# Attention kernel on one NeuronCore: another place for the full-array matmul, another order of SyncE's transfers

## The chip, the cores and the metric

The kernel runs on one core of a Trainium2 chip. The metric is the device time of one execution in microseconds (us), the median of the runs shown. Engines are named as the profile does: PE is TensorE (PEld its weight loads), DVE VectorE, ACT ScalarE, POOL GpSimd, SP SyncE, which here issues nearly all DMA transfers (its queue is SPq).

## The reference, cut to what matters

An image tensor `x` of 8 x 128 x 32 x 32 goes through six blocks, each added to its input: window attention with a depthwise convolution, a gated convolution, attention over all tokens, a mixture of experts with GELU, local attention, a mixture of experts with SiLU. The change touches the first and the third:

```python
# window attention: for each of two shifts and each of two halves of the channels
qw = _to_windows(q, nh, hs, nw, ws, HEADS) * scale      # windows of 128 tokens, 8 heads of 8
attn = softmax(einsum('whqc,whkc->whqk', qw, kw))
ow = einsum('whqk,whkc->whqc', attn, vw) + lw
...
# token attention: 1024 tokens, 16 heads of 8
attn = softmax(einsum('bhqd,bhkd->bhqk', q, k))
out = einsum('bhqk,bhkd->bhqd', attn, v)
return out.reshape(b, n, c) @ w_proj + b_proj
```

## The kernel before, in words

Each block is a stage with a barrier behind it. In both attention stages every engine runs its own program written out by hand, and semaphores tie them together; nothing reorders the work. The heads lie in four row groups of 32 partitions (`j` = 0 to 3), so that four small matmuls can run side by side.

**Window attention** (`window_attention`) works on 8 images of four stacks (`u` = 0 to 3; a stack is one shift and one half of the channels), each stack of four steps (`n`), 16 steps an image. **Token attention** (`token_attention`) has 8 images of eight groups (`g`) of eight steps, 64 steps an image. A step of TensorE's program is, in both:

- wait for `st_free[0]` (ScalarE has read the first score buffer); the full-array matmul `fill_array` (L368), 128 x 128 weights, 512 columns, whose result is thrown away: it is written to the half of the score buffer `st_ps` that real scores overwrite next;
- scores of the first pair of row groups (L558 in window attention, L945 in token attention), then maxima scores of two row groups for a stack or group two ahead (L542, L932), each waiting for a free one of the three buffers of `mx_ps` (`mx_free`);
- in one step of each stack or group the transpose of the split maxima (L548, L937);
- wait for `st_free[1]`; scores of the second pair; two more maxima scores;
- the values matmuls of the step before (L571, L959).

ScalarE takes two exponentials a step (L643, L1048) and now and then copies finished outputs (L636, L1032). VectorE takes four reductions a step (L667, L1073), copies the transposed maxima to `mT` (L671, L1082), in token attention reduces them once more (L1078), and inverts the denominators (`invert`, L678 and L1088). GpSimd splits the maxima (`split_max`), expands the values (`expand_v`), and adds finished images to `X` (`finish`, `normalise`, `add`).

The order around the change, in the window attention's SyncE program, one round for each stack `u`: `load_den` (L467, the denominators of the stack before, after waiting for ScalarE's copy), `load_qk` (L453, four transfers of 192 KB for the next image's stack `u-1`), a wait for VectorE's copy of the turned maxima, `load_rows` (L461, two transfers that put them under the queries of the stack after this one; TensorE waits for them at that stack's first step, `rows_loaded`), `regroup` (L476, eight transfers of finished outputs), `load_v` (L457). In rounds 1 and 3 `spread` follows: it waits for `invert`, stores the inverses to DRAM (L484), waits, and reads them back to many partitions (L488, two transfers of 256 KB). In token attention the reciprocal of the image before stands after step 4 of VectorE's program:

```python
if n == 4 and kind != "first":
    invert(i - 1)
```

Of the kernel before, what the change touches and what calls it, by code (L numbers as in the profile page):

```python
# [365 lines left out]
def fill_array(nc, out, ident, rows):  # L366

    nc.tensor.matmul(out, ident[:], rows, start=True, stop=True)  # L368
# [8 lines left out]
def window_attention(chip, X, qk_scr, v_scr, d_scr, ident, identf):  # L377
# [11 lines left out]
    U, S, STEPS, TURN = 4, 2, 16, 1  # L389
# [25 lines left out]
    with chip.stage() as ctx:  # L415
# [19 lines left out]
        rows_loaded, v_loaded, den_loaded, rb_loaded, regrouped, st_ready, st_free = ([chip.sem(s) for _ in range(2)] for s in (  # L435
            "rows_loaded", "v_loaded", "den_loaded", "rb_loaded", "regrouped", "st_ready", "st_free"))
# [11 lines left out]
        with nc.Block() as block:  # L448
            @block.sync
            def _(sp):  # L450
                def load_qk(i, u):
                    for j in range(4):
                        sp.dma_start(QK[32 * j:32 * j + STACK, u].rearrange("p o s n -> p o (s n)"),  # L453
                                     qk_scr[i, u, :, :, j].rearrange("o r s n -> r o (s n)")).then_inc(qk_loaded[u], 16)

                def load_v(i, u):
                    sp.dma_start(VS[:, u % 2], v_scr[i, u]).then_inc(v_loaded[u % 2], 16)  # L457

                def load_rows(u):
                    for c in range(2):  # L460
                        sp.dma_start(QS[STACK + c:C:32, u].rearrange("j s n -> j (s n)"),  # L461
                                     mT[64 * c:64 * c + 64, u % 2]).then_inc(rows_loaded[u % 2], 16)

                def load_den(i, u):

                    sp.wait_ge(o_free, i * STEPS + (4 * u + 5))
                    sp.dma_start(DEN[:, u // 2, u % 2], OR[D:C:32, u % 2].rearrange("j s n -> j (s n)")).then_inc(den_loaded[u % 2], 16)  # L467

                def regroup(i, u):

                    sp.wait_ge(x_done, i * 2 + (u // 2 + 2))
                    sp.wait_ge(o_free, i * STEPS + (4 * u + 5))
                    for j in range(4):
                        for s in range(2):
                            at = 64 * (u % 2) + 2 * j + s
                            sp.dma_start(ON[at:64 * (u % 2) + 64:8, u // 2], OR[32 * j:32 * j + D, u % 2, s]  # L476
                                         ).then_inc(regrouped[u % 2], 16)

                def spread(i, h):

                    count = i * 2 + (h + 2)
                    sp.wait_ge(x_done, count)
                    sp.wait_ge(inverted, count)
                    sp.dma_start(d_scr[i, h].rearrange("a p n -> p a n"), RD[:]).then_inc(rd_stored, 16)  # L484
                    sp.wait_ge(rd_stored, i * 32 + (16 * h + 32))
                    for part in range(2):
                        src = d_scr[i, h, part].rearrange("(s a) n -> s (a n)", s=8)
                        sp.dma_start(RB[64 * part:64 * part + 64, h],  # L488
                                     src.unsqueeze(0).to_broadcast([D] + list(src.shape))).then_inc(rb_loaded[h], 16)

                sp.wait_ge(ones_set, 1)
                load_qk(0, 0)
                load_v(0, 0)
                load_qk(0, 1)
                load_v(0, 1)
                load_qk(0, 2)
                load_qk(0, 3)
                sp.wait_ge(mx_free, 20 + 1 + 3)
                load_rows(0)
                sp.wait_ge(va_done, 1)  # L500
                load_v(0, 2)

                def image(i, kind):
                    for u in range(U):
                        if u:
                            load_den(i, u - 1)
                        elif kind != "first":
                            load_den(i - 1, 3)
                        if u == 0 and kind != "first":
                            load_qk(i, 3)  # L510
                        if u and kind != "last":
                            load_qk(i + 1, u - 1)
                        if kind != "last" or u < 3:
                            sp.wait_ge(mx_free, i * PER + (LEAD + MX[kind]["turn", u, TURNS[u][-1]] + 1 + 3))
                            load_rows((u + 1) % 4)
                        if u:
                            regroup(i, u - 1)
                        elif kind != "first":
                            regroup(i - 1, 3)
                        if kind != "last" or u < 1:  # L520
                            sp.wait_ge(va_done, i * U + (u + 2))
                            load_v(i + (u + 3) // 4, (u + 3) % 4)
                        if u == 3:
                            spread(i, 0)
                        if u == 1 and kind != "first":
                            spread(i - 1, 1)

                periods(sp, image)
                load_den(LAST, 3)
                regroup(LAST, 3)  # L530
                spread(LAST, 1)

            @block.tensor
            def _(pe):
# [15 lines left out]

                def scores(n, a):
                    u, s = n // 4, n // 2 % 2
                    if a == 0:
                        fill_array(nc, st_ps[:, a, 1], ident, KS[:, u, s, 0:HALF])
                    for w in range(4):
                        at = slice((n % 2 * 4 + w) * C, (n % 2 * 4 + w + 1) * C)
                        for e in range(2):
                            mm = nc.tensor.matmul(st_ps[:, a, e, w * C:(w + 1) * C], rows(KS, u, s, 2 * a + e, ROWS)[:, at],  # L558
                                                  rows(QS, u, s, 2 * a + e, ROWS)[:, at], start=True, stop=True)
                    mm.then_inc(st_ready[a], 1)  # L560
# [215 lines left out]
def token_attention(chip, X, dram, qk_scr, v_scr, d_scr, ident, identf, bias):  # L776
# [13 lines left out]
    STEPS = G * KT  # L790
# [25 lines left out]
    with chip.stage() as ctx:  # L816
# [19 lines left out]
        rows_loaded, v_loaded, regrouped, st_ready, st_free = ([chip.sem(s) for _ in range(2)] for s in (  # L836
            "rows_loaded", "v_loaded", "regrouped", "st_ready", "st_free"))
# [11 lines left out]
        with nc.Block() as block:  # L849
# [75 lines left out]
            def _(pe):  # L925
# [13 lines left out]

                def scores(n, a):  # L940
                    g, kt = n // KT, n % KT
                    if a == 0:
                        fill_array(nc, st_ps[:, a, 1], ident, KS[:, g // 2, 0:HALF])
                    for e in range(2):
                        mm = nc.tensor.matmul(st_ps[:, a, e], rows(KS, g // 2, 2 * a + e, ROWS)[:, kt * C:(kt + 1) * C],  # L945
                                              rows(QS, g // 2, 2 * a + e, ROWS)[:, g % 2 * HALF:(g % 2 + 1) * HALF],
                                              start=True, stop=True)
                    mm.then_inc(st_ready[a], 1)
# [112 lines left out]
            def _(v):  # L1061
# [42 lines left out]
                def image(i, kind):  # L1104
                    def ahead(n, pair):
                        for j in pair:
                            use = LEAD + MX[kind][n, j]
                            v.wait_ge(mx_ready, i * PER + (use + 1))
                            reduce_scores(n // KT, n, j, use % 3)

                    for n in range(STEPS):
                        g = n // KT
                        with_max = kind != "last" or n < STEPS - 16
                        if with_max:
                            if n % KT == 0:
                                v.wait_ge(max_taken, i * G + (g + 1))
                            ahead(n, (2, 3))
                        if n % KT == 0 and (kind != "last" or g < G - 1):
                            take_max(g + 1, i * PER + (LEAD + 33 * g + 3))
                        if n % KT == TURN and (kind != "last" or g < G - 1):  # L1120
                            use = LEAD + MX[kind]["turn", g]
                            if kind != "first" or g:
                                v.wait_ge(rows_loaded[(g + 1) % 2], i * 128 + ((g + 1) // 2 * 32))
                            v.wait_ge(mx_ready, i * PER + (use + 1))
                            copy_turned(g + 1, use % 3)
                        if with_max:
                            ahead(n, (0, 1))
                        if n == 4 and kind != "first":
                            invert(i - 1)

                periods(v, image)
# [1112 lines left out]
```

## Time and profile before

| | us |
|---|---|
| median of 3 runs | 4210.65 (4209.47 to 4216.52) |
| profiled execution, its own time | 4210.06 |
| its span | 4208.3 |
| window attention, first to last steps | 334 to 820 of the span |
| token attention, first to last steps | 1173.5 to 2696 |

| engine | busy us | share |
|---|---|---|
| PE | 3396.0 | 81% |
| DVE | 2493.0 | 59% |
| ACT | 1934.1 | 46% |
| POOL | 862.6 | 20% |

A busy time counts an engine's instructions, not its waits; matmul ends are modelled, so a busy PE is not PE at its peak. In the costliest groups a row gives an instruction's line, engine, operation, output and inputs, count, busy time and mean, then the idle time of the engine before it and what ended that. Timelines give start and length; "x4" merges neighbours of one kind, whose length is from the first start to the last end. PEclk is the clock that TensorE was granted, as a share of 2.4 GHz.

### The profile page before, as it was taken

What the parts mean: (1) busy time and instruction counts of PE and PEld (TensorE: products, weight loads), DVE (VectorE), ACT (ScalarE), POOL (GpSimd) and SP (SyncE); (2) the same over time, 40 slices, a digit from 0 to 9 for tenths busy, and PEclk for the clock granted to TensorE, in tenths of its full rate; (3) what the DMA queues carried; (4) which work ended last, traced back from release to release, by engine and by line L of the source; (5) the groups of instructions that cost most, each with busy time, mean ns of one, the idle gap of its engine ahead of it and who ended that gap; (6) DMA issues with size and microseconds to landing.
All of it is one profiled execution on the core that took longest, in us unless ns stands there. A gap on an engine that the chain in (4) does not pass through costs nothing. (4 is left out here: it accounts for less than half of the span.)

```text
span 4208.3 us, 66480 instructions
## 1 busy us (share of the span) xinstructions
PE 3396.0 (81%) x24463; PEld 1527.2 (36%) x24463; DVE 2493.0 (59%) x4082; ACT 1934.1 (46%) x2321; POOL 862.6 (20%) x866
## 2 busy tenths in 40 slices
PE   6988777557687777777777777779978659999999
PEld 4655455324211111111111111253366524444444
DVE  3227667465588888888888888344367523333333
ACT  1215666512156666666666666533333213223332
POOL 0001333300000000000000000004400225555555
PEclk9997878878789999999999999979998779999999
DMA  4444454300400000000000000014400122322221
GB/s 138 132 120 95 108 113 109 84 1 6 174 11 14 20 18 22 20 14 20 17 22 15 20 15 15 19 34 153 138 1 0 42 78 80 97 89 84 85 82 47
DMA packets 137544, 247.17 MB, mean 59 GB/s; under 512 B 34808, under 2 KB 47264, under 8 KB 136800
## 3 DMA queue, kind: packets, MB, share of 16 engines
q1 hardware_dynamic: 137312, 243.98, 20.5%
q8 instruction: 157, 2.57, 0.3%
q14 instruction: 75, 0.61, 0.0%
HBM read 171.55 MB, written 56.62 MB: 54 GB/s over the span
## 5 line engine op out<-in xcount | busy, mean ns | idle before, releaser
L1073 DVE TENSOR_REDUCE mxv<-mx_ps 128x1 f32<-128x512 f32 x2048 | 1279.6, 682 | 240.7 <-PE mx_ps L932 240.6
L1048 ACT ACTIVATE PT<-st_ps 128x1024 f32<-128x1024 f32 x1024 | 992.5, 1021 | 450.2 <-PE st_ps L945 444.4
L932 PE MATMUL mx_ps<-KS,QS 24*128 24x512 f16 x2048 | 538.0, 391 | 318.0 <-DVE mxv L1073 300.4
L1921 DVE TENSOR_TENSOR u<-h_ps,s 128x512 f32<-128x512 f32 x352 | 243.5, 692 | 541.2 <-ACT s L1899 492.8
L959 PE MATMUL o_ps<-PT,VA 128*32 128x512 f32 x4096 | 547.2, 606 | 1.1 <-ACT PT L1048 0.9
L1951 POOL TENSOR_TENSOR hg<-u,gb 128x512 f32<-128x512 f32 x352 | 451.6, 1285 | 392.6 <-DVE u L1921 300.2
L1899 ACT ACTIVATE s<-h_ps 128x512 f32<-128x512 f32 x352 | 210.2, 597 | 586.9 <-PE h_ps L1875 586.9
L667 DVE TENSOR_REDUCE mxv<-mx_ps 128x4 f32<-128x512 f32 x512 | 319.9, 683 | 150.3 <-PE mx_ps L542 139.2
L1883 PE MATMUL y_ps<-hg,m_w 128*128 128x512 f32 x704 | 360.7, 596 | 56.4 <-POOL hg L1951 56.4
L932 PEld LDWEIGHTS mx_ps<-KS,QS 24*128 24x128 f16 x2048 | 136.9, 91 | 568.3 <-DVE mxv L1073 530.7
L945 PE MATMUL st_ps<-QS,KS 26*128 26x512 f16 x2048 | 326.9, 382 | 1.0 <-ACT PT L1048 0.2
L643 ACT ACTIVATE PT<-st_ps 128x1024 f32<-128x1024 f32 x256 | 249.5, 1025 | 78.7 <-PE st_ps L558 70.6
L363 POOL TENSOR_TENSOR mt<-nm,less 128x16 f32<-128x16 f32 x64 | 13.9, 218 | 1291.9 <-DVE nm L1078 1291.9
L1873 PE MATMUL h_ps<-xh,m_wh 128*128 128x512 f16 x704 | 268.2, 381 | 9.6 <-DVE xl L1914 8.7
L1874 PE MATMUL h_ps<-xl,m_wh 128*128 128x512 f16 x704 | 267.9, 381 | 0.0
L1875 PE MATMUL h_ps<-xs,m_wl 128*128 128x512 f16 x704 | 267.8, 380 | 0.0
L542 PE MATMUL mx_ps<-QK 24*128 24x128 f16 x2048 | 163.4, 244 | 81.4 <-DVE mxv L667 59.7
L368 PEld LDWEIGHTS st_ps<-KS,ident 128*128 128x128 f16 x512 | 48.9, 95 | 438.7 <-issue 409.8
L368 PE MATMUL st_ps<-KS,ident 128*128 128x512 f16 x512 | 200.0, 391 | 9.9 <-ACT TX L1038 8.4
L363 POOL TENSOR_TENSOR VA<-VS,unit 128x512 f32<-128x512 f32 (+1 forms) x64 | 53.0, 827 | 672.4 <-DMA VS<-v 606.0
L1883 PEld LDWEIGHTS y_ps<-hg,m_w 128*128 128x128 f32 x704 | 132.0, 190 | 118.5 <-issue 51.9
L571 PE MATMUL o_ps<-PT,VA 128*32 128x128 f32 x4096 | 161.9, 306 | 4.3 <-ACT OR L636 2.3
(228 smaller groups left out, 4172.9 us busy)
## 6 DMA issues: line engine op xcount, KB each, us to landing
gb<-g SPq DMA_DIRECT2D x64, 512.0 KB, 3.7
gb<-g SPq DMA_DIRECT2D x16, 2048.0 KB
QK<-qk SPq DMA_DIRECT2D x128, 192.0 KB
qk<-hl SPq DMA_DIRECT2D x80, 256.0 KB, 3.3
RB<-d SPq DMA_DIRECT2D x48, 256.0 KB, 3.4
qk<-hl SPq DMA_DIRECT2D x64, 128.0 KB, 3.3
v<-vs SPq DMA_DIRECT2D x32, 256.0 KB
VS<-v SPq DMA_DIRECT2D x32, 256.0 KB, 3.1
```

The source lines that it names most:

```text
L643: nc.scalar.activation(PT[:, n % 2, 2 * a:2 * a + 2], st_ps[:, a], ACT.Exp, scale=SCALE).then_inc(st_free[a], 1)
L667: nc.vector.tensor_reduce(mxv[:, u % 2, j, n // 2 % 2, at:at + 4], mx_ps[:, slot].rearrange("p (w k) -> p w k", w=4), AX.X, ALU.max).then_ ...
L932: nc.tensor.matmul(mx_ps[:, use % 3, :], rows(QS, g // 2, j, STACK)[:, t * C:(t + 1) * C], rows(KS, g // 2, j, STACK)[:, half * HALF:(half ...
L945: mm = nc.tensor.matmul(st_ps[:, a, e], rows(KS, g // 2, 2 * a + e, ROWS)[:, kt * C:(kt + 1) * C], rows(QS, g // 2, 2 * a + e, ROWS)[:, g ...
L959: mm = nc.tensor.matmul(o_ps[32 * j:32 * j + 32, :], VA[:, g // 2 % 2, kt, j, :], PT[:, n % 2, j, :], start=(kt == 0), stop=(kt == KT - 1))
L1048: nc.scalar.activation(PT[:, n % 2, 2 * a:2 * a + 2], st_ps[:, a], ACT.Exp, scale=1.0 / SHIFT ** 2).then_inc(st_free[a], 1)
L1073: nc.vector.tensor_reduce(mxv[:, g % 2, j, t, half:half + 1], mx_ps[:, slot], AX.X, ALU.max).then_inc(mx_free, 1)
L1873: nc.tensor.matmul(out, wh[:, m, c, :], xh[:, s], start=True, stop=False)
L1874: nc.tensor.matmul(out, wh[:, m, c, :], xl[:, s], start=False, stop=False)
L1875: mm = nc.tensor.matmul(out, wl[:, m, c, :], xs[:, s], start=False, stop=True)
L1883: nc.tensor.matmul(y_ps[:, s], w2[:, c, :], hg[:, m % HG_SLOTS], start=(c == 0), stop=(c == CHUNKS - 1)).then_inc(y_steps, 1)
L1951: nc.gpsimd.tensor_tensor(hg[:, n % HG_SLOTS], u[:, n % H_SLOTS], gb[:, s, tile], ALU.mult).then_inc(gated, 1)
```

## The change

Three edits. In both attentions `fill_array` is issued for the second score pair (`a == 1`) instead of the first, so it now waits for `st_free[1]` and stands behind the first pair, its maxima scores and the transpose. In window attention SyncE's round now begins with a wait for the scores of the step that last reads the stack (`st_ready[1]`), then fetches the stacks, then the maxima rows, and only then the denominators and outputs, whose waits on ScalarE stand behind. In token attention the reciprocal moves from step 4 to step 6.

```diff
@@ window_attention, SyncE
                 def image(i, kind):
                     for u in range(U):
-                        if u:
-                            load_den(i, u - 1)
-                        elif kind != "first":
-                            load_den(i - 1, 3)
+                        if i or u:
+                            sp.wait_ge(st_ready[1], i * STEPS + 4 * u)
                         if u == 0 and kind != "first":
                             load_qk(i, 3)
                         if u and kind != "last":
@@ -514,8 +512,10 @@
                             load_rows((u + 1) % 4)
                         if u:
+                            load_den(i, u - 1)
                             regroup(i, u - 1)
                         elif kind != "first":
+                            load_den(i - 1, 3)
                             regroup(i - 1, 3)
@@ window_attention and token_attention, TensorE, scores(n, a)
-                    if a == 0:
+                    if a == 1:
@@ token_attention, VectorE
-                        if n == 4 and kind != "first":
+                        if n == 6 and kind != "first":
                             invert(i - 1)
```

The order of TensorE's instructions in an ordinary step of token attention (st_ps are scores, mx_ps maxima scores, o_ps values; L368 is the full-array matmul), before:

```order
L368 MATMUL st_ps<-KS,ident 128x512
L945 MATMUL st_ps<-QS,KS 128x512 x2
L932 MATMUL mx_ps<-KS,QS 128x512 x2
L945 MATMUL st_ps<-QS,KS 128x512 x2
L932 MATMUL mx_ps<-KS,QS 128x512 x2
L959 MATMUL o_ps<-PT,VA 32x512 x4
```

and now:

```order
L945 MATMUL st_ps<-QS,KS 128x512 x2
L932 MATMUL mx_ps<-KS,QS 128x512 x2
L368 MATMUL st_ps<-KS,ident 128x512
L945 MATMUL st_ps<-QS,KS 128x512 x2
L932 MATMUL mx_ps<-KS,QS 128x512 x2
L959 MATMUL o_ps<-PT,VA 32x512 x4
```

The full-array matmul moved from between the values and the first scores to between the two pairs. SyncE's queue in window attention, from the first spread on (DEN are denominators, QK<-qk stacks, QK<-mT maxima rows, ON outputs, VS values, d and RB the inverses' way through DRAM), before:

```order
L484 DMA d<-RD 128x2x64
L488 DMA RB<-d 64x1x1024 x2
L467 DMA DEN<-OR 128x1x64
L453 DMA QK<-qk 24x2x2048 x4
L461 DMA QK<-mT 4x16x128 x2
L476 DMA ON<-OR 8x1024 x8
L457 DMA VS<-v 128x512
L467 DMA DEN<-OR 128x1x64
L453 DMA QK<-qk 24x2x2048 x4
```

and now:

```order
L484 DMA d<-RD 128x2x64
L488 DMA RB<-d 64x1x1024 x2
L453 DMA QK<-qk 24x2x2048 x4
L461 DMA QK<-mT 4x16x128 x2
L467 DMA DEN<-OR 128x1x64
L476 DMA ON<-OR 8x1024 x8
L457 DMA VS<-v 128x512
L453 DMA QK<-qk 24x2x2048 x4
```

The denominators moved behind stacks and maxima rows; the stacks still follow the spread.

## Rows read from the trace of the kernel before

**Rows 1.** Page, part 5: xcount | busy us, mean ns | idle before, releaser.

```profile
L1073 DVE TENSOR_REDUCE mxv<-mx_ps 128x1 f32<-128x512 f32 x2048 | 1279.6, 682 | 240.7 <-PE mx_ps L932 240.6
...
L932 PE MATMUL mx_ps<-KS,QS 24*128 24x512 f16 x2048 | 538.0, 391 | 318.0 <-DVE mxv L1073 300.4
```

**Rows 2.** Window, then token attention: busy us (x), PEclk, DMA share, GB/s.

```profile
334.00:820.00 486.00, 374.37 (x8235) 247.69 (x8236) 318.65 (x536) 323.38 (x384) 161.44 (x187) 0.84 0.46 101
1173.50:2696.00 1522.50, 1211.86 (x8734) 292.26 (x8733) 1251.92 (x2120) 1037.45 (x1095) 92.97 (x234) 0.99 0.07 17
```

**Rows 3.** Timeline of PE, one step of token attention: start us, us, engine, line.

```profile
2007.17 0.39 PE L945 MATMUL st_ps<-QS,KS 26*128 26x512 f16 x2
...
2007.41 0.38 PE L945 MATMUL st_ps<-QS,KS 26*128 26x512 f16 x2
2008.39 0.38 PE L932 MATMUL mx_ps<-KS,QS 24*128 24x512 f16 x1 [0.60 <-DVE mxv L1073]
2008.70 1.06 PE L959 MATMUL o_ps<-PT,VA 128*32 128x512 f32 x8
2009.70 0.39 PE L368 MATMUL st_ps<-KS,ident 128*128 128x512 f16 x1
2010.02 0.39 PE L945 MATMUL st_ps<-QS,KS 26*128 26x512 f16 x2
```

**Rows 4.** Timeline of DVE and ACT in the same step.

```profile
2007.64 2.48 DVE L1073 TENSOR_REDUCE mxv<-mx_ps 128x1 f32<-128x512 f32 x4 [0.36 <-PE mx_ps L932]
2010.49 0.69 DVE L1073 TENSOR_REDUCE mxv<-mx_ps 128x1 f32<-128x512 f32 x1 [0.36 <-PE mx_ps L932]
...
2007.66 1.94 ACT L1048 ACTIVATE PT<-st_ps 128x1024 f32<-128x1024 f32 x2 [0.91 <-PE st_ps L945]
```

**Rows 5.** Timeline of PE, window attention, first matmul of four odd stacks.

```profile
410.44 0.61 PE L368 MATMUL st_ps<-QK,ident 128*128 128x512 f16 x1 [5.15 <-DMA QK<-mT]
...
474.09 0.61 PE L368 MATMUL st_ps<-QK,ident 128*128 128x512 f16 x1 [4.18 <-DMA QK<-mT]
...
505.24 0.61 PE L368 MATMUL st_ps<-QK,ident 128*128 128x512 f16 x1 [4.60 <-DMA QK<-mT]
...
784.19 0.61 PE L368 MATMUL st_ps<-QK,ident 128*128 128x512 f16 x1 [3.29 <-DMA QK<-mT]
```

**Rows 6.** Timeline of PE, a token step with the transpose of maxima.

```profile
2002.10 0.38 PE L932 MATMUL mx_ps<-KS,QS 24*128 24x512 f16 x1 [0.34 <-DVE mxv L1073]
```

**Rows 7.** Timeline of DVE, token attention, step 4 of an image.

```profile
1959.95 0.94 DVE L1088 RECIPROCAL RD<-DEN 128x128 f32<-128x128 f32 x1
```

**Rows 8.** Timeline of POOL, token attention, step 8 of that image.

```profile
1970.81 0.22 POOL L363 TENSOR_TENSOR mt<-nm,less 128x16 f32<-128x16 f32 x1 [1.59 <-DVE nm L1078]
```

**Rows 9.** Timeline of SyncE's DMA queue, window attention, odd stack after the wait.

```profile
479.30 0.60 SPq L467 DMA_DIRECT2D DEN<-OR  x1
479.94 1.74 SPq L453 DMA_DIRECT2D QK<-qk  x4
481.73 1.16 SPq L461 DMA_DIRECT2D QK<-mT  x2
482.99 4.92 SPq L476 DMA_DIRECT2D ON<-OR  x8
...
491.02 1.27 SPq L488 DMA_DIRECT2D RB<-d  x2
```

**Rows 10.** Timeline of DVE, window attention, copy of turned maxima.

```profile
481.01 0.21 DVE L671 COPY mT<-mx_ps 128x128 f16<-128x128 f16 x1
```

**Rows 11.** Start of token attention: PE's timeline, the stretch around it.

```profile
1177.53 0.61 PE L368 MATMUL st_ps<-KS,ident 128*128 128x512 f16 x1 [1.25 <-ACT PT L1048]
1178.07 0.61 PE L945 MATMUL st_ps<-QS,KS 26*128 26x512 f16 x2
...
1181.90 0.61 PE L368 MATMUL st_ps<-KS,ident 128*128 128x512 f16 x1
...
1174.00:1184.00 10.00, 7.78 (x35) 1.39 (x34) 6.77 (x13) 6.01 (x6) 1.22 (x4) 0.50 0.01 2
```

More of the change, by code:

```diff
@@ L941, in scores @@
                     g, kt = n // KT, n % KT
-                    if a == 0:
+                    if a == 1:
                         fill_array(nc, st_ps[:, a, 1], ident, KS[:, g // 2, 0:HALF])
```

## The prediction

> **What bounds the kernel now.** I read the costliest groups of the page first, then the busy time of the two attention stages, then the timeline of single steps, engine by engine; shares of the whole span say little here, since each stage has another limit. In token attention VectorE looks like the bound: 2048 reductions keep it busy 1279.6 us, but it is idle 240.7 us more, nearly all of it for TensorE's maxima scores, while TensorE in turn waits 318.0 us, mostly for VectorE [rows 1]. Two engines that wait for each other mean a loop, so the stage has to be read as one. Over the stage TensorE is busy 1211.86 and VectorE 1251.92 of 1522.5 us, and the DMA engines 0.07 [rows 2].
>
> The loop stands in the timeline of one step [rows 3, 4]. VectorE's first reduction starts at 2007.64; at its end it frees the buffer that the fourth maxima matmul waits for (2008.39, TensorE idle 0.60 before it). The values matmuls follow at 2008.70, the full-array matmul at 2009.70, the first scores at 2010.02, and the reduction of their neighbours starts at 2010.49. So the loop is 0.75 + 0.31 + 1.00 + 0.32 + 0.47 = 2.85 us, and the reader is to see that 0.32 of it is the full-array matmul, and that four reductions need 2.48 and leave 0.36 idle. ScalarE's two exponentials take 1.94, idle 0.91: not the bound.
>
> In window attention (486 us, DMA share 0.46, granted clock 0.84 against 0.99 in token attention [rows 2]) a second limit shows. Every odd stack of four steps begins with a wait for the maxima rows' DMA: 5.15, 4.18, 4.60 and 3.29 us at 410.44, 474.09, 505.24 and 784.19 [rows 5]. From the first to the last of these are twelve pairs of stacks, 373.75 us, 31.15 each.
>
> **The change, part by part.** *Full-array matmul in the second pair, token attention.* The same 512 matmuls are issued. Ahead of the first pair its 0.32 leaves the loop, which becomes 0.75 + 0.31 + 1.00 + 0.47 = 2.53. It goes where TensorE has its 0.60 of idle time: the second pair starts 0.24 after the first now (2007.41 against 2007.17), and would start about 0.64 after it (0.32 for four matmuls, by the step from 2008.39 to 2008.70, and 0.32 for the full-array one). The matmul behind it ends issuing near 0.97, and the fourth maxima matmul waits until 1.22 anyhow [rows 3]. So 0.25 us is left, and the cover is that wait for VectorE. In the step with the transpose the maxima matmuls of the second pair still wait for VectorE (0.34 idle at 2002.10 [rows 6]), so the 0.32 leaves there too. VectorE's own floor is next: 2.48 for four with the ends overlapping, below 2.53. Its idle time per step falls from 0.36 to 0.04. Steps with maxima: 8 x 64 - 16 = 496. Gain 496 x 0.32 = **159 us**.
>
> The array is split in another way before and after the moved matmul, and there is now one such change more per step. The rows: with the full-array matmul between other shapes nothing but its own 0.32 shows [rows 3]. The Trainium skill, TensorEngine Tiling (Array Packing), section Key Properties, says that a change of tiling mode drains TensorE; this speaks against the change, and were a drain to cost a further 0.32, its sum would be 0.07 less gain per step, 124 us in this part. The sum here goes by the rows, and the two ends are the whole 0.32 on each step and 0.22, if 0.1 us beyond the spare 0.25 comes up: 159 and 109 us. I take 159, since the row nearest to it (0.32 behind the full-array matmul) has no such excess.
>
> The 16 steps without maxima at the stage's end are set by ScalarE (1.94 for two exponentials [rows 4]) and TensorE together; the second exponential's buffer is now waited for 0.32 earlier in TensorE's order. Bounds 0 and +0.2 each; 1 us taken.
>
> *Reciprocal at step 6 instead of 4, token attention.* It takes 0.94 us on VectorE, behind four reductions [rows 7], and had the idle 0.36 of two steps to hide in; in a loop with 0.04 idle it costs about 0.35 more, 7 images, 2.5 us. Its readers: SyncE's spread, then GpSimd's multiplication, then GpSimd's split of maxima. GpSimd was free 1.59 us before the split could start at 1970.81 [rows 8], that is 9.3 us after the reciprocal's start. Now the split's input comes only about 4.7 us after that start (0.94, four reductions of step 7, two of step 8) instead of 10.9, so the split runs 4.6 us late; three operations of some 0.3 later it is done, about 0.7 us before its transpose wants it (two and a half loops of 2.53 after the input). Nothing on the path, but little spare. Token attention together: 159 - 1 - 2.5 = **155 us**.
>
> *SyncE's new order, window attention.* For an odd stack's rows the chain is [rows 9, 10]: wait over at 474.09, copy of the turned maxima ends at 481.22, rows of the next stack issued at 481.73, then eight output transfers from 482.99, the store of the denominators, and their broadcast (512 KB) at 491.02; behind it in the queue the next denominators, 768 KB of stacks and the odd stack's maxima rows, which end the next wait at 505.24 [rows 5], 14.22 after 491.02. The last piece is data in one queue: the 1280 KB ahead of the rows stay ahead of them, since the spread still comes first. So fetching stacks early shortens only what comes before. There the stacks (issued 479.94, now 9 us earlier) are out of the way of the even stack's rows, which go when the copy is done. Two steps at the low clock lose the full-array matmul's 0.54 each (1177.53 to 1178.07 at granted clock 0.50 [rows 11]), so the copy ends 6.05 after the wait instead of 7.13. Then 0.1 + 1.26 rows + 0.64 denominators, now behind them, + 8.03 to the broadcast = 16.1 instead of 16.93. Without denominators between broadcast and stacks the data may end 0 to 0.6 earlier; 0.3 taken. A pair of stacks becomes 16.1 + 13.9 = 30.0 instead of 31.15: 12 x 1.15 = 13.8. The other steps are not held by this wait: some 14 before 410.44 at 0.32, 4.5; those after 784.19, 1.7. Together **20 us**. Ends: 7, if data end later by what SyncE gains, and 45, if half of the waits vanish (12 x about 2). Where steps get shorter inside a held pair, the wait of about 4.6 grows instead, to about 6.
>
> Denominators are fetched some 4 us later in the even case; their readers come a full stack later. Nothing.
>
> **Sum.** 155 + 20 = 175 us. The profiled execution has a span of 4208.3 and its own time 4210.06 us, 1.8 around it; the median is 4210.65, 0.6 more. Forecast: 4210.65 - 175 = **4035 us**, rounded.
>
> **Rivals.** *B, drains eat a part.* The second pair is held up past its 0.25 of cover and each step loses 0.1: 4035 + 50 = 4085. For it: three neighbours in other shapes. Against it: the row at 2010.02.
> *C, the loop closes elsewhere.* The full-array matmul now waits for the second exponential of the step before. That ends 2.43 after the first scores start (0.49 + 1.94), the matmul stands at 2.53 + 0.32, so 0.42 is spare; were it binding, token attention would gain nothing: 4190.
> *D, slower.* The clock. When TensorE is granted 0.50 (1.2 GHz of 2.4) a token step lasts 4.37 us (1177.53 to 1181.90 [rows 11]), so 3.83 without the full-array matmul in the loop, 1.3 more than 2.53. If the new place let the granted clock fall, 135 of 496 steps would eat the 175; half of the steps give 4035 + 322 = 4357. For it: clock 0.84 in window attention, where TensorE waits, and waits there get longer. Against it: the same columns in less time, at 0.99. The Trainium skill, TensorE: Matmul & The Clock Gate, section "What's actually happening", has activity release the throttle; by it D would not come.
> *E, only the token part.* The window part gives nothing, as its waits grow by all that is saved: 4055, inside the range. That the change doesn't do what it says can be left out: the order of TensorE's instructions shows it in every step.
>
> **Numbers.** Forecast 0.76; E 0.08; B 0.07; C 0.03; D 0.06. The range takes the window part's upper end of 45 (4010) and reaches B (4085), rounded outwards for both together: 4010 to 4090. About 0.2% (8.4 us) is what a measurement of this kernel can tell from no change. Faster: all of forecast, E, B and most of C, 0.93; within it 0.01; slower 0.06.
>
> **What would show it.** Token steps 2.53 apart; VectorE's idle time before L1073 down from 240.7 to under 60; the full-array matmul directly behind the first maxima pair; TensorE's wait before the fourth maxima matmul about 0.2 instead of 0.60. In window attention pairs of 30 us, waits of 5 to 7 us for the rows still there, broadcast 16.1 after each. Wrong if token steps stay above 2.65 (B), if TensorE waits for ScalarE there (C), or if the granted clock in token attention is under 0.95 (D).

## The result and the profile after

The changed kernel takes 4032.6 us (median of 4 runs, 4027.78 to 4042.45) against 4212.34 us of the kernel before, measured again beside it: a ratio of 0.9574, 95% interval 0.9557 to 0.9590, so 180 us or 4.3% faster. The forecast was 4035, range 4010 to 4090.

| | before | after |
|---|---|---|
| span of the profiled execution | 4208.3 | 4026.0 |
| window attention, first to last scores matmul | 481.9 | 449.9 |
| token attention, first to last scores matmul | 1520.3 | 1366.5 |

By the profiles token attention gives 154 us and window attention 32, and the rest of the kernel is some 4 longer. The profiled execution is the fastest of the four, 5 us under their median; of the 180 us by the medians some 26 are left beside token attention's 154, if that stage was the same in all four.

The page's groups, then the two stretches of rows 2 (columns as there):

```profile
L1073 DVE TENSOR_REDUCE mxv<-mx_ps 128x1 f32<-128x512 f32 x2048 | 1276.9, 683 | 88.8 <-PE mx_ps L932 70.6
...
L932 PE MATMUL mx_ps<-KS,QS 24*128 24x512 f16 x2048 | 613.3, 394 | 114.0 <-DVE mxv L1073 96.6
```

```profile
334.00:786.00 452.00, 371.31 (x8216) 242.08 (x8218) 317.15 (x534) 317.89 (x384) 161.05 (x187) 0.82 0.52 109
1142.00:2509.00 1367.00, 1249.56 (x8733) 293.88 (x8736) 1247.70 (x2117) 1036.00 (x1095) 92.25 (x234) 0.99 0.07 19
```

Against [rows 1, 2]: VectorE's idle time before its reductions fell from 240.7 to 88.8 us at nearly the same busy time (1279.6 and 1276.9), TensorE's wait from 318.0 to 114.0, and the granted clock of token attention stayed at 0.99. The step itself, TensorE's timeline (start us, us):

```profile
1996.41 0.39 PE L945 MATMUL st_ps<-QS,KS 26*128 26x512 f16 x2
1996.42 0.39 PE L932 MATMUL mx_ps<-KS,QS 24*128 24x512 f16 x2
1996.74 0.39 PE L368 MATMUL st_ps<-KS,ident 128*128 128x512 f16 x1
1997.07 0.39 PE L945 MATMUL st_ps<-QS,KS 26*128 26x512 f16 x2
1997.07 0.38 PE L932 MATMUL mx_ps<-KS,QS 24*128 24x512 f16 x1
1997.63 0.38 PE L932 MATMUL mx_ps<-KS,QS 24*128 24x512 f16 x1 [0.17 <-DVE mxv L1073]
1997.94 1.06 PE L959 MATMUL o_ps<-PT,VA 128*32 128x512 f32 x8
1998.94 0.39 PE L945 MATMUL st_ps<-QS,KS 26*128 26x512 f16 x2
```

From 1996.41 to 1998.94 it is 2.53 us, where [rows 3] have 2.85. VectorE's first reductions of this step and of the next start at 1996.88 and 1999.40 with 0.04 idle before each, as forecast. Scores follow the values matmuls after 1.00, as the full-array matmul did before; the full-array matmul stands at +0.33, the second pair at +0.66 (0.64 forecast), and the fourth maxima matmul still waits, 0.17 instead of 0.60.

In window attention the wait at odd stacks is still there (first matmul of the stack, now a scores matmul), and SyncE's queue behind one of them reads:

```profile
402.74 0.29 PE L558 MATMUL st_ps<-QK 26*128 26x128 f16 x2 [4.53 <-DMA QK<-mT]
...
519.42 0.29 PE L558 MATMUL st_ps<-QK 26*128 26x128 f16 x2 [5.58 <-DMA QK<-mT]
...
752.04 0.52 PE L558 MATMUL st_ps<-QK 26*128 26x128 f16 x4 [2.70 <-DMA QK<-mT]
```

```profile
518.96 1.19 SPq L453 DMA_DIRECT2D QK<-qk  x3
525.50 1.22 SPq L461 DMA_DIRECT2D QK<-mT  x2
526.76 0.86 SPq L467 DMA_DIRECT2D DEN<-OR  x1
527.73 4.92 SPq L476 DMA_DIRECT2D ON<-OR  x8
...
533.25 0.40 SPq L484 DMA_DIRECT2D d<-RD  x1
535.92 1.25 SPq L488 DMA_DIRECT2D RB<-d  x2
```

The stacks go out before the wait has ended at 519.42, the maxima rows 6.08 after it (525.50; 7.64 in [rows 5, 9]), the broadcast 16.5 after it instead of 16.93. From 402.74 to 752.04 twelve pairs take 349.3 us, 29.1 each, where [rows 5] have 31.15.

### The profile page after: what moved, and what is told of

Read it like the earlier page. It is cut to its first block and busy times, and to the rows that moved or that the text cites. A ratio compares the mean times of both kernels' runs of the same rounds, so it can differ in the third digit from the quotient of the medians.

```text
span 4026.0 us, 66483 instructions
## 1 busy us (share of the span) xinstructions
PE 3440.5 (85%) x24463; PEld 1530.3 (38%) x24463; DVE 2489.7 (62%) x4082; ACT 1927.2 (48%) x2321; POOL 860.5 (21%) x866
## 5 line engine op out<-in xcount | busy, mean ns | idle before, releaser
L1073 DVE TENSOR_REDUCE mxv<-mx_ps 128x1 f32<-128x512 f32 x2048 | 1276.9, 683 | 88.8 <-PE mx_ps L932 70.6
L932 PE MATMUL mx_ps<-KS,QS 24*128 24x512 f16 x2048 | 613.3, 394 | 114.0 <-DVE mxv L1073 96.6
L945 PE MATMUL st_ps<-QS,KS 26*128 26x512 f16 x2048 | 400.4, 387 | 9.2 <-ACT TX L1038 8.5
L945 PEld LDWEIGHTS st_ps<-QS,KS 26*128 26x128 f16 x2048 | 96.5, 91 | 558.2 <-issue 479.7
L363 POOL TENSOR_TENSOR mt<-nm,less 128x16 f32<-128x16 f32 x64 | 13.8, 216 | 1113.0 <-DVE nm L1078 1113.0
L368 PE MATMUL st_ps<-KS,ident 128*128 128x512 f16 x512 | 201.0, 393 | 1.6 <-ACT PT L1048 0.9
```

What stands on the lines that cost most here:

```text
L932: nc.tensor.matmul(mx_ps[:, use % 3, :], rows(QS, g // 2, j, STACK)[:, t * C:(t + 1) * C], rows(KS, g // 2, j, STACK)[:, half * HALF:(half ...
L1073: nc.vector.tensor_reduce(mxv[:, g % 2, j, t, half:half + 1], mx_ps[:, slot], AX.X, ALU.max).then_inc(mx_free, 1)
```

## The experiments

Times are medians in us. Each ratio is against the kernel before, measured beside it on the same chip: 4211.55 with the first four kernels (the matmul alone, SyncE's order alone, the reciprocal, two full-array matmuls), 4217.26 with the four that leave the full-array matmul out or move the broadcast, 4211.88 with three full-array matmuls and with the best of both, 4216.57 with four. These differ by up to 6 us, so variants from different chips are compared by their ratios, and by single stages of their profiles. The length of a stage is from its first to its last scores matmul.

### The matmul alone

SyncE's order and the reciprocal as before; in both attentions:

```diff
-                    if a == 0:
+                    if a == 1:
                         fill_array(...)
```

> The full-array matmul in the second pair in both attentions, SyncE's order and the reciprocal as before. My theory: token attention shortens by 0.32 us in 496 steps, 155 to 159 us, whatever SyncE does in the other stage; window attention gains 4.5 + 1.7 us in steps that no transfer holds, and about 0.5 us in each of twelve held pairs, since SyncE still puts denominators and stacks ahead of the maxima rows: 12 us. Together about 4045 us. Rival (SyncE's order gives nothing, all gain is the matmul's): the same time as the full change, 4033.

Measured: 4046.4, ratio 0.9604 (0.9574 to 0.9633). Of the 180 us the matmul gives 165. Token attention is that of the full change to 1 us (1367.5 against 1366.5), so the remaining 14 us lie in window attention, where the same twelve pairs take 30.7 us each in this kernel and 29.1 in the full change: that is SyncE's order. The forecast for this kernel (4045) held.

### SyncE's order alone

The full change with `fill_array` back in the first pair and the reciprocal at step 4.

> SyncE's new order alone, full-array matmul in the first pair, reciprocal at step 4. My theory: the turned maxima come no earlier, so the rows are issued 0.4 us earlier at most and the broadcast is behind denominators as before; gain 0 to 6 us, 4206 to 4212, and token attention unchanged at 1520 us from its first to its last full-array matmul. Rival (earlier stacks take the wait of 4.2 to 5.2 us away): up to 12 x 4.5 = 54 us, 4158.

Measured: 4205.8 against 4211.55 (10 and 13 runs), ratio 0.9972 (0.9955 to 0.9990). Token attention lasts 1520.2 us, as before (1520.3). The medians differ by 6 us, and the ratio's interval allows 4 to 19, so as much as forecast (0 to 6) or a little more, and far from the 54 of the rival; the two parts add up to the whole within the intervals.

### The reciprocal back at step 4

```diff
-                        if n == 6 and kind != "first":
+                        if n == 4 and kind != "first":
                             invert(i - 1)
```

> The full change but with the reciprocal of token attention at step 4 again. My theory: the reciprocal costs VectorE its 0.94 us at either place and its inputs landed long before; 4033 within 2 us. Rival (the move to step 6 hides a wait for the denominators' transfer): slower by 5 us or more, with VectorE idle before L1088. A third way, that step 6 runs close to the split that the transpose of step 11 needs, would make this kernel faster by up to 5 us.

Measured: 4034.0, ratio 0.9581 (0.9555 to 0.9608). The move changes nothing that can be measured. In both kernels the step with the reciprocal lasts 3.19 to 3.20 us, 0.67 over its neighbours; in the kernel before it was 3.20 too, but only 0.35 over them.

### The full-array matmul twice, three and four times

Only in token attention, in the second pair:

```diff
                     if a == 1:
                         fill_array(...)
+                        fill_array(...)
```

> The full change with the full-array matmul issued twice in the second pair, in token attention only. My theory: of the wait before the fourth maxima matmul 0.25 us is left by my count; a second one takes 0.22 to 0.32, so it fits nearly and the steps stay at 2.53 to 2.60 us: 4033 to 4068. Rival (every full-array matmul costs its 0.32 wherever it stands): 2.85 us a step, 4033 + 159 = 4192.

> The full change with the full-array matmul issued three times in the second pair, token attention only. With two, TensorE's wait before the fourth maxima matmul is used up (15.6 us left in the whole stage against 96.6 with one). Theory (cover runs out, then each counts in full): the third lengthens the step by its 0.22 us of streaming, 2.53 to about 2.74: 4032 + 496 x 0.21 = 4136. Rival (VectorE sets the step, not the loop through TensorE): 4032 to 4050.

> The full change with the full-array matmul issued four times in the second pair, token attention only. With three, TensorE is never idle in a step: 0.33 first pair, 0.76 full-array, 0.44 second pair, 1.00 values, 2.53 together. Theory (the cover held two more of 0.22 us, not one, and is now used up): the fourth lengthens every one of 496 steps by 0.22, to 2.75 us: 4030 + 109 = 4139. Rival (something else still leaves room, as with the third): 4030 to 4050.

Measured: twice 4031.5 (ratio 0.9570, 0.9544 to 0.9595), three times 4030.5 (0.9571, 0.9549 to 0.9593), four times 4071.2 (0.9651, 0.9625 to 0.9676). For two the steps stayed at 2.53 us as expected and the time came out 1.5 us under the range's lower end; for three the expectation failed and its rival's time came out, give or take 2 us, though not by its reason (with four the steps do get longer at the same work of VectorE); for four the direction was right and the size wrong: 34 us by the ratios and 40 by token attention (1406.6 against 1366.5 with three) instead of 109. TensorE's timeline of one step with three, then with four:

```profile
2002.09 0.39 PE L947 MATMUL st_ps<-QS,KS 26*128 26x512 f16 x2
2002.10 0.39 PE L932 MATMUL mx_ps<-KS,QS 24*128 24x512 f16 x2
2002.42 0.82 PE L368 MATMUL st_ps<-KS,ident 128*128 128x512 f16 x3
2003.18 0.39 PE L947 MATMUL st_ps<-QS,KS 26*128 26x512 f16 x2
2003.18 0.51 PE L932 MATMUL mx_ps<-KS,QS 24*128 24x512 f16 x2
2003.62 1.06 PE L961 MATMUL o_ps<-PT,VA 128*32 128x512 f32 x8
2004.62 0.39 PE L947 MATMUL st_ps<-QS,KS 26*128 26x512 f16 x2
```

```profile
2002.34 0.39 PE L948 MATMUL st_ps<-QS,KS 26*128 26x512 f16 x2
...
2002.66 1.04 PE L368 MATMUL st_ps<-KS,ident 128*128 128x512 f16 x4
2003.63 0.39 PE L948 MATMUL st_ps<-QS,KS 26*128 26x512 f16 x2
2003.64 0.39 PE L932 MATMUL mx_ps<-KS,QS 24*128 24x512 f16 x2
2003.96 1.06 PE L962 MATMUL o_ps<-PT,VA 128*32 128x512 f32 x8
2004.96 0.39 PE L948 MATMUL st_ps<-QS,KS 26*128 26x512 f16 x2
```

With three, the second pair and its maxima need 0.44 from 2003.18 to the values, since the last maxima matmul starts only at 2003.30; with four they need 0.33 from 2003.63, four matmuls side by side. Each full-array matmul more costs 0.22 (0.76 for three, 0.97 for four). So the three other matmuls of the second pair needn't be out before the fourth is released, 1.21 us after the step's first matmul (2002.09 to 2003.30): all four can start then. The room between the first pair's end (0.32) and that point is 0.89, less the first full-array matmul's 0.32: 0.57 us left, not 0.25. Two more fit (0.44), the third overruns by 0.09: steps of 2.62 instead of 2.53, 496 x 0.09 = 45 us, where 40 were measured.

### Without the full-array matmul

`fill_array` is left out of one stage; its result is overwritten, so the computation is complete.

> The full change without the full-array matmul in token attention (its result is overwritten, so nothing is left out of the computation). The loop of values, first pair, reduction and fourth maxima matmul no longer holds it, so by the loop alone the steps stay at 2.53 us: 4032. My theory of its purpose: it keeps TensorE's granted clock up; without it the clock falls to 0.50 in part of the stage, where steps last 3.83 us, and the run is slower, anywhere up to 4032 + 496 x 1.3 = 4677, with the granted clock of the stage under 0.95. Rival (it is dead weight): 4032 within 5 us.

> The full change without the full-array matmul in window attention. Theory: the pairs of stacks are held by the transfers (29.1 us each), so a faster step gains nothing, and a lower clock costs where it lasts through a pair: 4032 to 4080. Rival (window attention is held by TensorE): 4010 or less.

Measured: without it in token attention 4625.6 (4581.87 to 4663.60), ratio 1.0997 (1.0945 to 1.1048); without it in window attention 4074.1, ratio 0.9671 (0.9639 to 0.9702). Both theories held. The stretches of the two stages in these kernels (token attention of the first, window attention of the second; a line ends with the granted clock, the DMA share and GB/s):

```profile
1155.00:3067.00 1912.00, 1719.46 (x8214) 249.43 (x8213) 1253.72 (x2115) 1032.96 (x1094) 92.52 (x234) 0.56 0.05 13
```

```profile
390.00:800.00 410.00, 374.28 (x6558) 265.92 (x6555) 269.19 (x451) 256.04 (x306) 143.64 (x161) 0.50 0.49 106
```

Token attention lasts 1914 instead of 1366 us at a granted clock of 0.56, though VectorE's work is the same: the steps are not lengthened by their contents but by the clock. In window attention the clock stays at 0.50 (1.2 GHz) all through the stretch shown, no stack waits for its rows any more there, and a pair of stacks takes 32.2 us, only 3 more than when it waits for transfers at the higher clock.

The full change shows the same in small, once, behind the step with the projection in the fifth image of token attention:

```profile
1850.00:1897.00 47.00, 42.22 (x299) 10.16 (x295) 42.03 (x72) 34.43 (x37) 4.23 (x8) 1.00 0.10 27
1897.00:1911.00 14.00, 14.00 (x65) 2.35 (x65) 9.21 (x18) 7.59 (x9) 0.65 (x3) 0.52 0.03 7
1911.00:1950.00 39.00, 36.06 (x258) 8.40 (x257) 37.85 (x64) 30.51 (x33) 4.23 (x8) 1.00 0.07 19
```

For some 14 us the clock is at 0.52 and steps last 3.83 us, the figure that the prediction worked out; this costs 4 us. It is no accident of one run. All six profiled kernels with one full-array matmul in token attention's second pair have such stretches, and each begins behind a projection step: one of 14 us here and without the full-array matmul in window attention, one of 37.5 us (12 us lost) with the reciprocal at step 4, two with the matmul alone, and in the next section three with the late broadcast and two with the early split. The two with it in the first pair (the kernel before and SyncE's order alone) have none, and neither have the four with two or more in the second pair, apart from the stage's first steps, which run at the lower level in all of them. TensorE waits 1.21 us for ScalarE at the projection in the kernel before as well, so the wait alone does not do it.

### The broadcast behind the maxima rows

The kernel before and the full change fetch 512 KB of inverses ahead of stacks and rows. Here SyncE stores the inverses where it did, and issues the broadcast in the next round:

```diff
                             load_rows((u + 1) % 4)
+                        if u == 0 and kind != "first":
+                            broadcast(i - 1, 0)
+                        if u == 2 and kind != "first":
+                            broadcast(i - 1, 1)
                         if u:
                             load_den(i, u - 1)
```

and in a second kernel GpSimd also splits the maxima before it finishes the image:

```diff
-                        if u % 2 == 0 and kind != "first":
-                            finish(i - 1, u // 2)
                         if kind != "last" or u < 2:
                             split_max(...)
+                        if u % 2 == 0 and kind != "first":
+                            finish(i - 1, u // 2)
```

> The full change, and in window attention the broadcast of the inverses (512 KB) is issued in the next round, behind stacks and maxima rows instead of ahead of them. Theory (the wait at odd stacks is for data queued ahead of stacks and rows): the queue ahead of the rows shrinks from 1280 to 768 KB and starts earlier, the wait of 5 to 7 us at twelve odd stacks shrinks or goes; but GpSimd's finish of the image then starts later and its split of the maxima stands behind it, which can become the next wait: 20 to 80 us faster, 3950 to 4010. Rival (the wait is SyncE's issue time, not data): within 5 us of 4032.

> As the kernel with the late broadcast, and GpSimd splits the maxima before it finishes the image. Theory: removes the wait that GpSimd's finish makes; pairs of stacks go from 29.1 towards the 22 us that eight unheld steps take, held at some 23.5 by the transfers: window attention 370 to 400 instead of 447 us, 3960 to 3985. Rival (the transfers as a whole bound the pair at about 29 us, whatever their order): 4032.

Measured: 4050.8 (ratio 0.9601, 0.9578 to 0.9624) and 3985.6 (0.9450, 0.9431 to 0.9469). The first is 18 us slower than the full change by the medians and 11 by the ratios, whose intervals just overlap; faster it is not, and its window attention lasts 470 us instead of 450. Its time went where the expectation had seen a danger, only that it took all of the gain and more. Waits of window attention in the first kernel, then in the second (who <- for whom: us in total, times, longest):

```profile
PEld mx_ps L555 <- POOL mp L743: 83.7, 12, 7.5
PE mx_ps L555 <- POOL mp L743: 81.6, 12, 7.3
```

```profile
PEld st_ps L565 <- DMA QK<-mT: 13.9, 9, 3.1
PE st_ps L565 <- DMA QK<-mT: 11.5, 7, 2.9
PEld mx_ps L555 <- POOL mp L743: 0.4, 1, 0.4
```

In the first no wait of TensorE for the maxima rows is left; instead the transpose waits twelve times, up to 7.3 us, for GpSimd's split, which stands behind `finish`. With the split ahead of `finish` that wait is gone as well, and the one for the rows, which lasts up to 7.1 us in the full change, is down to at most 2.9. Window attention takes 405 us instead of 450, a pair of stacks 25.3: more than the 23.5 and the 370 to 400 us expected, so the time ends at the upper end of its range (3985).

What the wait is made of shows in part. An odd stack starts 9.6 us (median) after its rows are issued in the full change, and 6.4 with the late broadcast, where TensorE never waits for them: so some 3 us of it went with the data ahead of them in the queue. But moving the broadcast takes another wait away, that of SyncE's queue for the store of the inverses to land, which stood ahead of broadcast, stacks and rows. In the full change, then with late broadcast and early split:

```profile
SPq L488 <- DMA d<-RD: 32.9, 15, 3.6
```

```profile
SPq L489 <- DMA d<-RD: 3.0, 3, 1.6
```

These 2.2 us a pair let stacks and rows go out earlier too. No kernel here keeps the one and drops the other, so their shares in the gain are not shown.

### The best of both

The last kernel with the full-array matmul twice in both attentions.

> The kernel with late broadcast and early split, with the full-array matmul issued twice in the second pair of both attentions. Theory: the second is hidden at the full clock, and more full-array work keeps the granted clock up through the short waits: the clock of window attention rises from about 0.90, and no stretch of token attention is at 0.50: 3965 to 3983. Rival (window steps have no room for a second, or it lengthens the steps at the low clock by 0.4 us): 3986 to 4010.

Measured: 3973.3 (5 runs, 3967.46 to 3974.56), ratio 0.9431 (0.9414 to 0.9447), the lowest of all, 60 us below the full change. Against the kernel without the second one it is 12 us lower by the medians, but 8 by the ratios, whose intervals overlap. Its two stages:

```profile
334.00:728.00 394.00, 358.03 (x8292) 221.62 (x8290) 316.84 (x534) 312.51 (x382) 160.00 (x186) 0.94 0.53 124
1091.00:2452.00 1361.00, 1325.12 (x9232) 296.70 (x9231) 1247.87 (x2118) 1037.09 (x1094) 92.26 (x234) 1.00 0.07 19
```

The clock of window attention is 0.94; it is 0.89 with the same order and one full-array matmul, and 0.82 in the full change, where the waits are longer too. That of token attention is 1.00, against 0.99 with one. In the profiles the second full-array matmul shortens window attention from 405 to 395 us and token attention from 1368 to 1363: more work on TensorE made both stages shorter there, though the runs' times alone don't settle it.

## Why the prediction was right

**The loop.** Token attention was forecast to gain 155 us and gained 154; its steps last 2.53 us as worked out from 0.75 + 0.31 + 1.00 + 0.47. The kernel with the matmul alone and the one with SyncE's order alone show that this is the matmul's, and only its. That the sum fits to 1 us is luck in part: the 154 hold a loss of 4 us to the clock that the sum didn't have. Where no stretch at the low clock came (two full-array matmuls, 1362.4 us) the gain is 158. The last 16 steps, put at 1 us of loss, last 31.5 us in both kernels. One of the signs was set wrongly too: VectorE's idle time was to fall under 60 us, but 240.7 less 496 x 0.32 is 82 by the prediction's own terms, and 88.8 were measured.

**The cover** was sized wrongly, on the safe side. The sum had 0.25 us left behind the moved matmul; it is 0.57, as the kernels with two, three and four show. The step at fault is "the matmul behind it ends issuing near 0.97": it took for granted that the second pair's other matmuls must be out before the fourth is released. It didn't change the sum, since one full-array matmul fits either way, but rival B's price (0.1 us a step beyond 0.25) rests on it: by 0.57 such a delay would still have been covered.

**The drains (rival B).** The Trainium skill, TensorEngine Tiling (Array Packing), section Key Properties, has a change of tiling mode drain the array. The traces fit it, with a small price: a full-array matmul between other shapes takes 0.32 us and a further one directly behind it 0.22, and the first pair with its maxima takes 0.33 when the full-array matmul follows (1996.41 to 1996.74) where the second pair followed it after 0.24 (2007.17 to 2007.41 in [rows 3]). So some 0.1 us goes with a change of shape, and the new order has one such change more. But the sum had taken 0.32 for both terms, so that 0.1 was in it, and no further cost appeared.

**The clock (rival D)** had the right price (3.83 us a step at 0.50), and its trigger is real: without the full-array matmul it comes nearly everywhere. Moving the matmul pulled it too, but only behind some projection steps, for 4 us here and up to 12 in the other kernels, and not for half of the steps; the prediction, which left it at nothing in its sum, was right to within that. By TensorE: Matmul & The Clock Gate of the Trainium skill, section "What's actually happening", activity releases the throttle. Taken as busy time, that would not tell the two kernels apart: without the full-array matmul TensorE was still busy in 1719 of 1912 us and was granted 0.56, with it in 1250 of 1367 us at 0.99. So the measurement decides, and the full-array matmul is what kept the clock up; whether a filler of another shape would do the same was not run.

**The second exponential (rival C)** did not bind: TensorE's idle time before token attention's L368 for ScalarE is 0.9 us in all 512.

**The reciprocal** costs 0.32 more a time than before, in seven images 2.2 us, where 2.5 were summed. Its place doesn't matter.

**Window attention** was forecast to gain 20 us and gained some 26 by the medians, 32 in the profiled execution. There the broadcast comes 16.2 us after the odd stack's start in the mean of the twelve pairs (16.5 in the rows above, forecast 16.1), but the next odd stack then starts after 11.7 to 13.5 us, 12.9 in the mean, where 13.9 had been taken; with the matmul alone it is 13.8. So the mis-sized term is the 0.3 us for data that end earlier without denominators between broadcast and stacks: it was about 1, and made 29.1 a pair instead of 30.0. And the first wait ends 7.7 us earlier (402.74 against 410.44) where 4.5 were summed; 1.4 of this is the stage's earlier start. Behind the last of these waits the 1.7 us summed came out. Both misses lie within the ends given. That the wait would stay held, and it grew: 49.8 us in all, up to 7.1 at once, against 39.3 and 5.4 in the kernel before.

What stays open is why the granted clock falls where it does, within window attention and behind some of the projections. It goes along with most of the spread of the times: in ten runs of the kernel with SyncE's order alone, 4189 to 4220 us, the two fastest were granted 0.93 over the whole kernel and the slowest 0.918. Where the stretches at 0.50 lie is known for one run of each kernel only.

## What to carry to other kernels

Where two engines each seem to wait for the other, write down the loop through both from one step of the timeline and ask of every instruction whether it is in it; a filler that is needed for the clock costs its full length in the loop and nothing two places further on. Size such a place by the last moment at which the work behind it can still start, not by when that work starts now. Where a wait for one small transfer is in truth a wait for what is queued ahead of it, move the large transfer, and look at once for what stood behind its consumer.

## What the runs showed of the hardware

In this kernel a filler of 128 x 128 weights and 512 columns decides which of its two levels TensorE's clock has: token attention with one to four in a step runs at 0.99 to 1.00, without one at 0.56, though TensorE is busy for 90% of that stage. I had expected part of the stage to fall to the lower level, but not nearly all of it. The filler's place counts a little too: with one, moved to the second pair, 3.4 to 37.5 us at a time were granted 0.50 behind a projection step in each of six profiles, with one in the first pair or several in the second in none. And four matmuls of 512 columns in the four row groups take 0.33 us together (2003.63 to 2003.96 with four full-array matmuls), hardly more than the 0.31 of a single one that was held back (1997.63 to 1997.94), while a full-array matmul behind another one costs 0.22.
